# Window attention and a residual projection: TensorE's extra matmuls placed ahead of the turn of a step, and the moments of x1 taken from carried totals and ScalarE's squares

## What is computed

```
x = x + attention(group_norm(x))
x = x + deformable_conv(group_norm(x))

group_norm(v): m = mean(group), s = var(group);  (v - m) / sqrt(s + 1e-5)

attention: windows of 16 x 16 pixels (256 tokens), 8 heads of 16 channels
  attn = softmax(q @ k.T * scale + bias)      # per window and head, 256 x 256
  out  = (attn @ v) -> windows back to pixels -> out @ proj_w.T + proj_b
```

## Time and profile before

| | us |
|---|---|
| median of 3 runs (lowest, highest) | 3146.19 (3132.41, 3151.75) |
| the profiled execution: time | 3148.91 |
| its span, first to last instruction | 3147.2 |
| busy in the span: TensorE, VectorE, ScalarE, GpSimd | 2708.4, 2685.1, 1789.2, 1268.0 |
| attention | about 85 to 1510 |
| residual projection of image 0, of image 1 | about 1525 to 1576, 2351 to 2400 |

### The profile page before, as it was taken

The page is one execution under the profiler, slowest core; times in us unless marked ns, Lnnn a source line. Parts: engine busy times, 40 slices in busy tenths (PEclk is TensorE's granted clock), DMA queues, the critical chain, the costliest instruction groups (busy, mean ns, idle before and its releaser), DMA issues.

```text
span 3147.2 us, 78097 instructions
## 1 busy us (share of the span) xinstructions
PE 2708.4 (86%) x22424; PEld 2186.9 (69%) x22424; DVE 2685.1 (85%) x6553; ACT 1789.2 (57%) x3476; POOL 1268.0 (40%) x1837
## 2 busy tenths in 40 slices
PE   1898989999999999998677999899867879999999
PEld 0565656666666666666566888888866778889888
DVE  3788888888888888888657999989987779999998
ACT  0788888888888888888142334333302333334331
POOL 3333333333333333332526344743640554554541
PEclk9999999999999999999888999999989899999999
DMA  7999998788788878887763454454444544444443
GB/s 184 168 157 169 157 166 131 145 138 147 134 151 142 142 145 139 146 134 139 219 190 103 140 151 140 126 159 136 116 128 145 171 126 127 137 130 126 135 114 110
DMA packets 429629, 453.44 MB, mean 144 GB/s; under 512 B 80781, under 2 KB 346397, under 8 KB 428420
## 3 DMA queue, kind: packets, MB, share of 16 engines
q1 hardware_dynamic: 414276, 442.74, 62.8%
q0 software_dynamic: 15168, 8.36, 2.2%
HBM read 294.58 MB, written 156.62 MB: 143 GB/s over the span
## 4 chain that ended last, share of the span: by engine, by line
DVE 26%; issue 10%; DMA 6%; PE 5%; DVEq 2%; POOL 2%; ACT 1%; SPq 0%; POOLq 0%; ACTq 0%
DVE prod L1734 19%; DMA vring<-vals 2%; DVE tt L1718 2%; DVE my L1713 2%; DMA vring<-attended 1%; PE sum_ps L1484 1%; DVE x L1745 1%; PE sum_ps L1532 1%; PE wt_ps L1462 1%; DVE x L1649 1%; DMA vals<-vring 1%; DVE reach L1670 1%; PE om_ps L1447 1%; DMA o_sel<-off_out,pos 1%; PE sum_ps L1433 1%
## 5 line engine op out<-in xcount | busy, mean ns | idle before, releaser
L755 ACT ACTIVATE prob<-sbias,nmax 128x256 f32<-128x256 f32 x2048 | 922.3, 501 | 179.7 <-DVE nmax L848 168.2
L848 DVE CUSTOM_DVE_ANT_0 sbias<-s_ps,nbias 128x256 f32<-128x256 f32 x2048 | 769.3, 419 | 215.9 <-PE s_ps L640 206.9
L1734 DVE TENSOR_TENSOR prod<-vring,wt_ps 128x1920 f32<-128x1920 f32 (+3 forms) x512 | 900.7, 1811 | 14.3 <-DMA vring<-vals 11.9
L1484 PE MATMUL sum_ps<-ident,prod 128*128 128x128 f32 x6400 | 750.3, 274 | 26.5 <-DVE prod L1734 26.0
L1484 PEld LDWEIGHTS sum_ps<-ident,prod 128*128 128x128 f32 x6400 | 718.1, 141 | 68.2 <-DVE prod L1734 43.3
L653 PE MATMUL pt_ps<-ident,prob 128*128 128x128 f32 x4096 | 640.2, 279 | 132.0 <-ACT prob L755 131.4
L653 PEld LDWEIGHTS pt_ps<-ident,prob 128*128 128x128 f32 x4096 | 454.3, 141 | 258.9 <-DVE probT L857 145.7
L1586 ACT ACTIVATE hat<-off,one_col 128x576 f32<-128x576 f32 x128 | 140.3, 1096 | 622.4 <-DVE tt L1718 622.4
L573 POOL CAST parts<-qk 128x1024 bf16<-128x1024 f32 x64 | 66.4, 1037 | 853.3 <-ACT qk L748 853.3
L640 PE MATMUL s_ps<-stack 96*128 96x256 bf16 x2048 | 396.2, 274 | 9.0 <-DMA stack<-parts_dram 8.1
L857 DVE COPY probT<-pt_ps 128x512 f32<-128x512 f32 x512 | 351.3, 686 | 1.8 <-PE pt_ps L653 1.8
(11 more groups left out here) (183 smaller groups left out, 3451.7 us busy)
## 6 DMA issues: line engine op xcount, KB each, us to landing
stack<-parts_dram SPq DMA_DIRECT2D x768, 128.0 KB, 7.3
vring<-vals SPq DMA_DIRECT2D x270, 320.0 KB
parts_dram<-parts SPq DMA_DIRECT2D x64, 768.0 KB, 3.3
off_out<-off SPq DMA_DIRECT2D x64, 432.0 KB
strips<-x SPq DMA_DIRECT2D x68, 256.0 KB, 3.6
far_sums<-nothing SPq DMA_DIRECT2D x64, 256.0 KB, 3.6
attended<-on SPq DMA_DIRECT2D x256, 64.0 KB
x<-x SPq DMA_DIRECT2D x64, 256.0 KB
```

Source lines behind the costliest of these rows:

```text
L755: ins = nc.scalar.activation(prob[:, n % 4, half, :], sbias[:, n % SBIAS, half, :], ACT.Exp, bias=nmax[:, n % SBIAS, half:half + 1], scale ...
L848: ins = nc.vector.tensor_tensor_reduce(out=sbias[:, n % SBIAS, half, :], in0=s_ps[:, n % 2, half, :], in1=nbias[:, h, half, :], scale=1.0, ...
L1484: mm = nc.tensor.matmul(sum_ps[:, par, r * H:(r + 1) * H], prod[:, r % 2, dx, dy * C:(dy + 1) * C], ident[:], start=(r + dx + dy == 0), st ...
L1734: nc.vector.tensor_tensor(prod[:, r % 2, first:last].rearrange("p a (t c) -> p (a t) c", c=CG), vring[:, at:at + wide].rearrange("p a (t c ...
```

## The change

In attention the `turn` of a TensorE step moves from directly behind the scores to the end of the step, behind the step's extras. Steps without extras keep their order. Nothing moves on the other engines. In the residual projection VectorE's add carries the tile's sum along (`tensor_tensor_reduce` in place of `tensor_tensor`), ScalarE squares the tile with a carried sum in place of `bn_stats`, and two short reductions and one scaling stand in place of `bn_aggr` and its two followers. The loops over tiles on ScalarE and VectorE are written out.

```diff
             def pair(p, par, first=False, left=AHEAD):
                 for n in range(SLOTS):
                     scores(p, n, par)
-                    if n >= T_LAG:
-                        turn(p, n - T_LAG)
-                    elif not first:
-                        turn(p - 1, n - T_LAG + SLOTS)
                     if n % 4 == 3:
...
                     if n == V_AT and left >= 1:
                         proj_v(p + 1, 1 - par)
+                    if n >= T_LAG:
+                        turn(p, n - T_LAG)
+                    elif not first:
+                        turn(p - 1, n - T_LAG + SLOTS)
...
+                for ai in range(NA):
+                    act.wait_ge(a_read, count(b * NA + ai + 2))
+                    if ai >= 3:
+                        act.wait_ge(sq_ready, count(b * NA + ai - 2))
+                    act.sem_inc(act_passed, 1)
+                    nc.scalar.activation(hat[:, ai % 3].rearrange("p r k -> p (r k)")[:, 0:COLS * W],
+                                         x1[:, ai * (COLS * W):(ai + 1) * (COLS * W)], ACT.Square,
+                                         accum_out=moments[:, 1, ai:ai + 1]).then_inc(sq_ready, 1)
...
-                        nc.vector.tensor_tensor(rows, sum_ps[:, par], rows, ALU.add).then_inc(a_read, 1)
-                        dve.wait_ge(a_read, count(a + 2))
-                        nc.vector.bn_stats(bn[:, bass.ds(ai, 1), :].rearrange("p a b -> p (a b)"), rows) \
-                          .then_inc(x1_ready, 1)
...
+                    nc.vector.tensor_tensor_reduce(out=rows, in0=sum_ps[:, ai % 2], in1=rows, scale=1.0, scalar=0.0,
+                                                   op0=ALU.add, op1=ALU.add,
+                                                   accum_out=moments[:, 0, ai:ai + 1]).then_inc(a_read, 1)
...
-                nc.vector.bn_aggr(mv[:], bn[:].rearrange("p a b -> p (a b)")).then_inc(g_step, 1)
...
+                nc.vector.tensor_reduce(mv[:, 0:1], moments[:, 0], AX.X, ALU.add).then_inc(g_step, 1)
+                dve.wait_ge(sq_ready, count(NA * (b + 1)))
+                dve.sem_inc(dve_passed, 1)
+                nc.vector.tensor_reduce(mv[:, 1:2], moments[:, 1], AX.X, ALU.add).then_inc(g_step, 1)
+                dve.wait_ge(g_step, count(3 * b + 2))
+                nc.vector.tensor_scalar(ex[:], mv[:], 1.0 / PIX, None, ALU.mult).then_inc(g_step, 1)
```

More of the change, by code:

```diff
@@ L934, in deformable @@
         x1 = sb("x1", [P, PIX])
-        bn = sb("d_bn", [P, PIX // 512, 6])
+        moments = sb("moments", [P, 2, H // COLS])
         mv = sb("d_mv", [P, 2])
@@ L1002, in deformable @@
         b_added = sem("b_added")
-        x1_ready = sem("x1_ready")
+        sq_ready = sem("sq_ready")
         g_step = sem("g_step")
@@ L1653, in _ @@
-                dve.wait_ge(x1_ready, count(NA * (b + 1)))
-                dve.sem_inc(dve_passed, 1)
-                nc.vector.bn_aggr(mv[:], bn[:].rearrange("p a b -> p (a b)")).then_inc(g_step, 1)
[L1656 to L1659, removed]
+                for ai in range(NA):
+                    a = b * NA + ai
+                    dve.wait_ge(a_done, count(a + ATTS))
+                    dve.wait_ge(b_added, count(a + 1))
+                    dve.sem_inc(dve_passed, 1)
+                    rows = x1[:, ai * (COLS * W):(ai + 1) * (COLS * W)]
+                    nc.vector.tensor_tensor_reduce(out=rows, in0=sum_ps[:, ai % 2], in1=rows, scale=1.0, scalar=0.0,
+                                                   op0=ALU.add, op1=ALU.add,
+                                                   accum_out=moments[:, 0, ai:ai + 1]).then_inc(a_read, 1)
@@ new lines, in _ @@
+                dve.wait_ge(a_read, count(NA * (b + 1) + 1))
+                dve.sem_inc(dve_passed, 1)
+                nc.vector.tensor_reduce(mv[:, 0:1], moments[:, 0], AX.X, ALU.add).then_inc(g_step, 1)
+                dve.wait_ge(sq_ready, count(NA * (b + 1)))
+                dve.sem_inc(dve_passed, 1)
+                nc.vector.tensor_reduce(mv[:, 1:2], moments[:, 1], AX.X, ALU.add).then_inc(g_step, 1)
+                dve.wait_ge(g_step, count(3 * b + 2))
+                nc.vector.tensor_scalar(ex[:], mv[:], 1.0 / PIX, None, ALU.mult).then_inc(g_step, 1)
```

## The result

The changed kernel takes **3264.24 us** (median of 4 runs, 3255.28 to 3266.16), the kernel before, run beside it, 3141.43 us (4 runs, 3132.41 to 3151.75). The ratio is **1.0383, 95% interval 1.0353 to 1.0412**: 3.8% slower. The profiled execution has a span of 3264.0 us against 3147.2 us before, 116.8 us more.

A forecast was written before the change was run, and what follows sets the result against it. No engine is full; attention is bound by a ring of waits among VectorE, ScalarE and TensorE. 3148.9 + 140 - 12 = 3277 us profiled, 3274 us as a median, 4.1% slower; range 3225 to 3345 us.

The forecast's parts named there:

- Term 1: Attention: the late turn lengthens the longest way round three engines' queues, pairs from 21.88 to 24.10 us, 140 us more.
- E to A: Attention, ScalarE: from the exp's start to its copy of an even step, 0.81 us.
- A to W: Attention: from the start of ScalarE's even-step copy to TensorE's weigh that waits for it, 0.64 us.
- W to T: Attention, TensorE: from the weigh to the turn now behind it, 1.01 us.
- T to D: Attention: from TensorE's turn to VectorE's copy of an odd step that waits for it, 0.70 us.
- D to B: Attention, VectorE: from its copy of an odd step to the next bias_max, 0.60 us.
- B to E: Attention: from VectorE's bias_max to ScalarE's exp that waits for it, taken as 0.85 us.
- Term 2: Residual projection: less VectorE work for the moments, mostly in image 1, saves 12 us (6 to 17).
- The table load: Residual's end: the new load behind ScalarE's last square is hidden before the Sqrt, with 0.8 us left.
- Rival 1: Attention: VectorE has slack, the delay stays on TensorE, 88 us more, 3222 us; chance 0.12.
- Rival 2: Attention: extras fill TensorE's wait for the exponentials, 126 us gained, 3008 us; chance 0.04.
- Rivals 3 and 4: Attention: more is pushed, 3350 us or more, chance 0.08; whole kernel: both parts cancel, no change, chance 0.03.

The follow-up runs named there:

- e3: Kernel before with only the weigh moved ahead of the turn in attention, other extras behind it, residual unchanged; 3266.17 us, ratio 1.0400 to the kernel before.
- e5: Turn late behind the extras, and ScalarE's odd-step copy put ahead of the exp; 3195.69 us, ratio 1.0164 to the kernel before.
- e6: Control: kernel before, turn first, with only ScalarE's odd-step copy put ahead of the exp; 3185.34 us, ratio 1.0129 to the kernel before.
- e7: Turn late behind the extras, plus one unused 512-element VectorE addition in step 3 of each pair; 3307.88 us, ratio 1.0539 to the kernel before.
- e8: Kernel before, turn first, plus one unused 512-element VectorE addition in step 3 of each pair; 3145.98 us, ratio 1.0004 to the kernel before.
- e2: Changed kernel with the turn put back right behind the scores, so the residual half alone; 3131.84 us, ratio 0.9963 to the kernel before.
- e9: Changed kernel's residual; weigh one step later, ahead of the turn, other extras behind it; 3133.32 us, ratio 0.9970 to the kernel before.
- e11: As e9, with the projections and their reads also two steps later, away from the weigh; 3051.75 us, ratio 0.9710 to the kernel before.
- e10: As e9, but with the weigh behind the turn of its new step; 3236.39 us, ratio 1.0307 to the kernel before.
- e4: Kernel before with turn_out and the projections moved ahead of the turn, the weigh behind it; 3173.86 us, ratio 1.0107 to the kernel before.

## Why the prediction was right

Forecast 3274 us, measured 3264.24, inside 3225 to 3345; slower, as said.

- **Term 1, the way round: right in its mechanism.** Every link was found. E to A 0.81 (0.81 forecast), A to W 0.62 (0.64), W to T 1.00 (1.01), T to D 0.79 (0.70), D to B 0.60 (0.60), B to E 0.80 (0.85). The quarters shown are 6.23 and 5.95 us where 6.16 and 5.89 were worked out, the pair 24.18 against 24.10. e3 shows that the weigh alone carries it, e5 and e6 that most of it hangs on the input's age, e7 and e8 that the way leads over VectorE.
- **Term 1, the size: 11 us too large.** 140 us were forecast, 129.15 measured. The mis-sized term is the pair of before. I took one distance of two starts, 21.88 us, and the mean over 28 pairs is 22.04; the first 16 pairs, in which the loop over the input's statistics runs alongside, take 22.45 us before and 24.15 after. That gives 16 x 1.70 + 47 x 2.14 = 128 us. T to D was mis-sized too: 0.70 for the 0.78 to 0.79 seen behind every late turn, 0.33 us in a pair. A third of it was made good by B to E, and half by luck, in the quarter from step 7 to 11, which took 6.00 us for 6.16. There VectorE goes from B(8) over norm to B(9) in 1.38 us (1019.16 to 1020.54 us) and not in the 1.55 of the earlier trace rows, in which norm's multiplication (1023.91 us) starts after 0.19 us of idle time. So 24.10 us wasn't the least that the order allows, as the prediction said, and 24.18 isn't as close a hit link by link as it looks.
- **Term 2: right.** 12 us forecast. The two residual stretches have 11.7 us less (0.87 for 1.3 forecast, 10.83 for 10.7), e2 has 12 us. Of image 1's 10.83 us, 0.89 are the end (4.44 us from the last add to the Sqrt before, 3.55 after), 9.4 are the 31 distances between adds (46.03 us before, 36.58 after), and the rest lies ahead of the first add. In part the sum is lucky: the 27 distances of the earlier trace rows gave 8.2 us, at 1.17 us each for the 1.10 that I took, and the first four, which I left out, gave 1.2. TensorE is the busiest engine there now, 9.57 of 10 us. From the last add to the small matmul it is 2.16 us (2.3 forecast).
- **The table load: hidden, as forecast.** It ends at 2519.15 and the Sqrt starts at 2519.83 for another reason, 0.68 us of room (0.8 forecast). The Trainium skill (ScalarE: Activation LUTs, What ACT_TABLE_LOAD costs) counts a drain of 1.38 us besides the 1.28 us of load. By it the load that starts at 2517.87 would have held the Sqrt until 2520.53, 0.7 us later than it came. The trace shows the load 0.02 us behind ScalarE's last instruction and the Sqrt at VectorE's release, so here the measurement decides against it. The prediction left out a second load, which stands ahead of the image's first square (1.28 us at 2480.46). It costs nothing at the end: the last square waited for its add, as its bracket says.
- **The rivals.** Rival 1, the delay stays on TensorE (3222 us): refuted by D's 184.6 us of waits for the turn, and by e7. Rival 2, the extras fill the wait: not in this change, since the copy comes too late. Nor was an input that is there enough, as the rival had it: e9's weigh finds its input, and e9 gains nothing. With the projections moved away as well, e11 has 82 us (against e9) of the gain that I had put at 126 us. Rivals 3 and 4 didn't occur.
- **What I had wrong in the experiments' expectations.** I took the order in which the inputs come for the only thing that counts (e9, e10), and left out how much stands between two scores. And I took the copy's place on ScalarE for free (e6).

What stays open: how e6's 39 us and e4's 31 us split over the links of the ring wasn't tried. Nor was e11's gain divided further: the projections' new places move their reads on ScalarE and VectorE and GpSimd's work as well, and no run moved these alone. Nor did any run move the projections in the order of before, so it isn't shown that the weigh's new place has a share in the gain.

## What to carry to other kernels

When engines wait for each other in a ring, cost a moved instruction by the longest way through the in-order queues: for each extra, ask whether its last input is older than the input of the work that it is put ahead of. If it is younger (here a copy behind the exp), the order can lose the extra's length and its wait on every engine down the ring. An old input alone wasn't enough here: with the weigh a step on, the time was that of e2 (3133.32 against 3131.84 us). The gain came when weigh and projection no longer shared a step (3051.75 us, against 3145.35 for the kernel before beside it). So look also at how much stands between two scores. Take the length of a period that is subtracted as a mean over many, since 0.16 us of it were 10 us here.

## What the runs showed of the hardware

ScalarE's sum along the row isn't free: each square of 512 elements takes 0.63 us, and an ACTIVATION_READ_ACCUMULATOR of 0.19 us stands behind it as an instruction of its own. On VectorE the add with carried sum takes 0.69 us, no more than the plain add of the earlier trace rows, and its read 0.08 us. And an instruction of 0.68 us on VectorE cost nothing measurable in e8 and 40 us in e7, in the same place of the same queue.
